# AdaLN layer with linear attention and top-2 MoE on one core: weights transposed on the host instead of on TensorE

## The reference, cut to what matters

```python
mod = (silu(c) @ wmod).reshape(4, 6, 1, -1)            # sa, ca, ga, sb, cb, gb
h = layernorm(x) * (1 + ca) + sa
QKV = einsum('bsd,ed->bse', h, W_in) + b_in            # W_in (768, 256)
Q, K = rope(Q), rope(K)
A = sum_s(K / |K| * V);  Y = A * Q @ W_out.T + b_out   # W_out (256, 256)
x = x + ga * (Y + h)
h = layernorm(x) * (1 + cb) + sb
probs = softmax(h @ router_w.T);  top 2 of 8 experts per token
out = sum_e comb[e] * ((silu(h @ Wg[e].T) * (h @ Wu[e].T)) @ Wd[e].T)   # Wg, Wu (704, 256), Wd (256, 704)
x = x + gb * (out + ...)
```

## Time and profile before

| what | value |
|---|---|
| times of three runs | 335.81, 335.94, 338.87 us |
| median | 335.94 us |
| span of the profiled execution | 338.7 us |
| the run nearest to that span | 338.87 us |
| PE, PE weight loads, DVE, ACT, POOL busy | 287.7, 196.3, 185.6, 134.1, 79.3 us |
| DMA | 33.34 MB in 25387 packets, mean 98 GB/s |

### The profile page before, as it was taken

The page is one execution under the profiler, slowest core; times in us unless marked ns, Lnnn a source line. Parts: engine busy times, 40 slices in busy tenths (PEclk is TensorE's granted clock), DMA queues, the critical chain, the costliest instruction groups (busy, mean ns, idle before and its releaser), DMA issues.

```text
span 338.7 us, 5051 instructions
## 1 busy us (share of the span) xinstructions
PE 287.7 (85%) x1466; PEld 196.3 (58%) x1467; DVE 185.6 (55%) x497; ACT 134.1 (40%) x325; POOL 79.3 (23%) x93
## 2 busy tenths in 40 slices
PE   3987799886956668999999999999999999999600
PEld 0644666775845335776777776666666666666400
DVE  1467743399368854766766763444444453444126
ACT  1273473653673055756474622223332222232000
POOL 1005544621100040022211222233222223311213
PEclk9999797999555557999999999999999999999955
DMA  7990342035353371564443110101110011100083
GB/s 247 373 291 3 132 142 85 0 90 168 87 163 116 105 219 32 154 175 140 134 154 118 31 33 32 33 20 50 28 35 31 23 31 30 44 16 0 2 261 111
DMA packets 25387, 33.34 MB, mean 98 GB/s; under 512 B 2193, under 2 KB 20276, under 8 KB 25368
## 3 DMA queue, kind: packets, MB, share of 16 engines
q1 hardware_dynamic: 22952, 27.85, 25.9%
q0 software_dynamic: 2208, 5.17, 5.3%
q10 hardware_dynamic: 208, 0.08, 0.1%
HBM read 28.86 MB, written 5.14 MB: 100 GB/s over the span
## 4 chain that ended last, share of the span: by engine, by line
PE 72%; DVE 15%; DMA 4%; ACT 3%; issue 2%; SPq 1%; POOL 0%; DVEq 0%; ACTq 0%
PE bank L750 25%; PE bank L777 19%; PE bank L561 7%; PE bank L763 5%; PE bank L631 3%; PE bank L644 3%; PE bank L551 2%; DMA W<-in_L_attn_W_in 2%; PE bank L670 2%; DMA W<-expert_parts 2%; DVE W L1097 1%; PE bank L704 1%; PE bank L738 1%; ACT W L838 1%; PE bank L570 1%
## 5 line engine op out<-in xcount | busy, mean ns | idle before, releaser
L750 PE MATMUL bank<-W,rows 128*128 x414 | 90.4, 368 | 1.1 <-DVE rows L1271 1.1
L777 PE MATMUL bank<-W,shared 128*128 (+1 forms) x276 | 69.2, 389 | 0.7 <-DVE shared L1307 0.7
L750 PEld LDWEIGHTS bank<-W,rows 128*128 128x128 f16 x414 | 40.8, 100 | 38.3 <-issue 3.6
L1282 DVE SCALAR_TENSOR_TENSOR shared<-bank,unscale,rows 128x256 f32<-128x256 f32 (+1 forms) x69 | 31.8, 461 | 53.5 <-ACT rows L945 53.4
L1381 POOL DMA_INDIRECT expert_parts<-shared,dest_i x23 | 23.3, 1014 | 149.4 <-DVE shared L1292 149.4
L777 PEld LDWEIGHTS bank<-W,shared 128*128 128x128 f32 (+1 forms) x276 | 48.2, 189 | 13.2 <-issue 8.6
L945 ACT ACTIVATE rows<-bank,unscale 128x256 f32<-128x256 f32 (+1 forms) x69 | 31.4, 454 | 45.8 <-PE bank L750 45.8
L1097 DVE SCALAR_TENSOR_TENSOR W<-bank,w_scale_bits,W 128x512 f16<-128x512 f32 (+1 forms) x48 | 33.4, 704 | 24.1 <-ACT W L853 23.8
L853 ACT ACTIVATE W<-bank,w_scale_bits 128x512 f16<-128x512 f32 (+1 forms) x48 | 30.4, 648 | 29.6 <-DVE w_scale_bits L1089 16.7
L561 PE MATMUL bank<-keep,staged 128*128 128x128 f32 x192 | 34.6, 310 | 8.0 <-DVE w_norm L1084 3.6
L561 PEld LDWEIGHTS bank<-keep,staged 128*128 128x128 f32 x192 | 26.5, 165 | 17.0 <-issue 4.9
(11 more groups left out here) (179 smaller groups left out, 322.5 us busy)
## 6 DMA issues: line engine op xcount, KB each, us to landing
staged<-in_L_ffn_Wd SPq DMA_DIRECT2D x8, 704.0 KB
staged<-in_L_ffn_Wg SPq DMA_DIRECT2D x8, 640.0 KB
staged<-in_L_ffn_Wu SPq DMA_DIRECT2D x8, 640.0 KB
W<-expert_parts SPq DMA_DIRECT2D x8, 256.0 KB, 4.6
W<-in_L_wmod SPq DMA_DIRECT2D x3, 512.0 KB, 8.1
token_rows<-rows SPq DMA_DIRECT2D x1, 1040.0 KB, 5.3
x<-in_L_attn_X SPq DMA_DIRECT2D x4, 256.0 KB, 9.0
W<-mod_rows SPq DMA_DIRECT2D x4, 256.0 KB, 4.1
```

The lines of the kernel that those rows point to most:

```text
L750: mm = pe.matmul(bank[2 + n][:, 0:2 * w], slot[:, kc * P:(kc + 1) * P], W1_16[:, bass.ds(e * (2 * W1_EXP) + at, 2 * w)], start=(k == 0), s ...
L777: mm = pe.matmul(bank[7][:, 0:D], actT[0:rows, fc * P:(fc + 1) * P], W2[0:rows, bass.ds(e * W2_EXP + fc * D, D)], start=(fc == 0), stop=(f ...
L1282: ve.scalar_tensor_tensor(act[:, n * PIECE:n * PIECE + w], bank[2 + n][:, w:2 * w], unscale[c % 2][:, 1:2], sig[:, n * PIECE:n * PIECE + w ...
```

## The change

The host now lays out all weights with the input dimension on the partitions, one contiguous run per partition. `w1[e]` holds gate and up of an expert together, 128 partitions of 2816 numbers (1.44 MB); it goes to one of two `staged` buffers. `w2[e]` (down, 0.79 MB) goes straight to its place in `W2`. Biases, router weights, condition and `wmod` come laid out too, so their transposes go, as does the `swap` matmul for the rotary pairs.

On PE only `norm(e)` is left of the groups. It is in step 1 and 2 between kv and q, in steps 6 and 7 between `th` and `r`, twice in the routing, and in tiles 2 and 3 between `down` and `turn_act`. ACT's `sum_squares(e)` is two instructions of 128x1408, its `high(e, m)` two of 128x704 from `staged`; DVE's `low(e, m)` is two of 128x704. Gate and up lie apart in `W1`, so the moving operand of a `gate_up` matmul is two runs of w columns instead of one run of 2w.

```diff
-STAGED = 4
+STAGED = 2
...
+            def load_w1(e):
+                if e >= STAGED:
+                    sp.wait_ge(s["lo_ok"], 2 * DC * (e - STAGED + 1))
+                sp.dma_start(staged[e % STAGED][:], w1_d[e]).then_inc(staged_in[e % STAGED], 16)
+            def load_w2(e):
+                wait_places(sp, e)
+                sp.dma_start(W2[:, e * W2_EXP:(e + 1) * W2_EXP], w2_d[e]).then_inc(w2_in[e], 16)
+            load_w1(0)
+            load_w1(1)
+            load_w2(0)
+            load_w2(1)
...
+            load_w2(2)
+            load_w2(3)
+            load_w1(2)
+            load_w1(3)
+            load_w2(4)
+            load_w2(5)
+            load_w1(4)
+            load_w1(5)
...
+            def norm(e):
+                pe.wait_ge(s["sumsq_ok"], 2 * (e + 1))
+                if e >= 2:
+                    pe.wait_ge(s["wscale_ok"], e - 1)
+                pe.matmul(bank[e % 2][:, 0:2], keep[:, C_ONE:C_ONE + P], sumsq[:, 2 * e:2 * e + 2],
+                          start=True, stop=True).then_inc(s["norm_done"], 1)
...
-                for g in step_slot(k, 1):
-                    turn(g)
+                if k in (1, 2):
+                    norm(k - 1)
                 for b in at_step(k, 1):                    # q
...
+                if k in (6, 7):
+                    norm(k - 4)
                 for b in at_step(k, 6):                    # r
...
                     mm.then_inc(s["cnt_done"], 1)
-                    for g in range(route_first, route_mid):
-                        turn(g)
+                    norm(4)
...
                     mm.then_inc(s["table_done"], 1)
-                    for g in range(route_mid, tiles_first):
-                        turn(g)
+                    norm(5)
...
                     for k, (slot, kc, part) in enumerate(terms):
-                        at = part * W1_EXP + kc * W1_COLS + 2 * PIECE * n
                         mm = pe.matmul(bank[2 + n][:, 0:2 * w], slot[:, kc * P:(kc + 1) * P],
-                                       W1_16[:, bass.ds(e * (2 * W1_EXP) + at, 2 * w)],
+                                       W1_pairs[:, bass.ds(e * 2 + part, 1), :, kc, n * PIECE:n * PIECE + w],
...
+                    pe.wait_ge(s["lo_ok"], 2 * DC * (c + 1))      # before gate_up of tiles 0 to 7
...
+            def high(e, m):                                       # ACT
+                sc.wait_ge(s["wscale_ok"], e + 1)
+                for kc in range(DC):
+                    at = m * W1_MAT + kc * F
+                    sc.activation(w1_part(e, 0, m, kc), staged[e % STAGED][:, at:at + F], ACT.Identity,
+                                  scale=w_scale[:, 2 * e + m:2 * e + m + 1]).then_inc(s["hi_ok"], 1)
...
-                for g in step_slot(k, 1):
-                    turn_out(g)
+                if k in (2, 3, 6, 7):                             # ACT, between ksq and q1
+                    high({2: 0, 3: 1, 6: 2, 7: 3}[k], 0)
...
+                if k in (2, 3, 6, 7):                             # ACT, after wA
+                    high({2: 0, 3: 1, 6: 2, 7: 3}[k], 1)
...
+                if k in (1, 5, 6, 9):                             # ACT, end of the step
+                    sum_squares({1: 1, 5: 2, 6: 3, 9: 4}[k])
             sc.wait_ge(s["sub_ok"], 1)
             sc.activation(expo[:], logit_less_max[:], ACT.Exp).then_inc(s["expo_ok"], 1)
+            sum_squares(5)
+            high(4, 0)
+            high(4, 1)
+            high(5, 0)
+            high(5, 1)
...
+                    if c in (1, 2):                               # ACT, tile c, after slots_out
+                        sum_squares(c + 5)
+                    if c in (3, 5):
+                        high(c // 2 + 5, 0)
...
+                if k in (3, 4, 7, 8):                             # DVE, between kv and q
+                    low({3: 0, 4: 1, 7: 2, 8: 3}[k], 0)
...
+                if k in (1, 2, 6, 7):                             # DVE, before y
+                    power_scale({1: 0, 2: 1, 6: 2, 7: 3}[k])
...
+                if k in (3, 4, 7, 8):                             # DVE, between diff and h2
+                    low({3: 0, 4: 1, 7: 2, 8: 3}[k], 1)
...
             routing_choice(ve, link)
+            power_scale(4)
             routing_places(ve, link)
             routing_table(ve, link)
-            for g in range(route_first, tiles_first):
-                turn_out(g)
+            power_scale(5)
+            low(4, 0)
+            low(4, 1)
...
+                if first and c in (0, 4, 6):                      # DVE, tile c, after slots_out
+                    low({0: 5, 4: 6, 6: 7}[c], 0)
...
                 ve.tensor_copy(actT[:, 0:4 * P], bank[5][:]).then_inc(s["actT_v"], 1)
+                if first and c in (0, 4, 6):
+                    low({0: 5, 4: 6, 6: 7}[c], 1)
```

More of the change, by code:

```diff
@@ L279, in layer @@
         staged_in = [sem(f"staged_in{r}") for r in range(STAGED)]
+        w2_in = [sem(f"w2_in{e}") for e in range(E)]
         xs_in = [sem(f"xs_in{r}") for r in range(4)]
@@ L283, in layer @@
         part_in = [sem(f"part_in{b}") for b in range(B)]
-        groups = [("w_in", None, n) for n in range(3)] + [("w_in_swapped", None, 0), ("w_out", None, 0)]
-        FIRST = len(groups)
-        groups += [("norm", 0, 0)]
-        for e in range(E):
-            groups += [("gate", e, n) for n in range(3)] + [("up", e, n) for n in range(3)]
-            groups += [("down", e, n) for n in range(3)] + [("norm", e + 1, 0)] * (e + 1 < E)
-        MATRIX = {"gate": 0, "up": 1, "down": 2}
-        STEPS = 10
@@ L320, in layer @@
-        for g in range(tiles_first, ALL_GROUPS):
-            group_bank[g] = (g - route_mid) % 2
-        def last_on_bank(g):
-            before = [h for h in range(g) if group_bank[h] == group_bank[g]]
-            return before[-1] if before else None
-        def tile_slot(i, c, n):
-            if not (isinstance(i, int) and i == 0 and c < len(TILE_GROUPS)):
-                return range(0)
-            at = tiles_first + sum(map(sum, TILE_GROUPS[:c])) + sum(TILE_GROUPS[c][:n])
-            return range(at, at + TILE_GROUPS[c][n])
@@ L335, in split @@
-        def split(g):
-            return groups[g][0] in ("gate", "up")
-        def by_act(g):
-            return split(g) or (g < FIRST and g % 2 == 0) or (groups[g][0] == "down" and g < tiles_first)
-        def by_dve(g):
-            return split(g) or not by_act(g)
-        def wait_turned(eng, upto):
-            eng.wait_ge(s["turn_act"], sum(by_act(g) for g in range(upto)))
-            eng.wait_ge(s["turn_dve"], sum(by_dve(g) for g in range(upto)))
-        def wait_out(eng, g):
-            by = by_dve if by_dve(g) else by_act
-            eng.wait_ge(s["turn_dve" if by_dve(g) else "turn_act"], sum(by(h) for h in range(g + 1)))
@@ L787, in tile_step @@
             def tile_step(i, c):
-                def turn_some(n):
-                    for g in tile_slot(i, c, n):
-                        turn(g)
                 if isinstance(i, int) and i == 0 and c < E:
-                    done = tile_slot(0, c, 0).start
-                    if c == 0:
-                        for h in range(route_first, route_mid):
-                            wait_out(pe, h)
-                    need = [g for g in range(done) if groups[g][0] in ("gate", "up") and groups[g][1] <= c
-                            or groups[g][0] == "down" and groups[g][1] < c]
-                    wait_turned(pe, need[-1] + 1)
-                gate_up(i, c, turn_some)
+                    pe.wait_ge(s["lo_ok"], 2 * DC * (c + 1))
+                gate_up(i, c)
                 if not (isinstance(i, int) and c == SLOT_TILES - 1):
@@ L843, in turn_out @@
-            def turn_out(g):
-                kind, e, n = groups[g]
-                if (kind, n) == ("down", 1) and e + 1 < E:
-                    sum_squares(e + 1, 1)
-                if split(g):
-                    if (kind, n) == ("gate", 0):
-                        sc.wait_ge(s["wscale_ok"], e + 1)
-                    sc.wait_ge(s["turn_done"], g + 1)
-                    src, hi, lo = split_views(g)
-                    c = 2 * e + MATRIX[kind]
-                    sc.activation(hi, src, ACT.Identity, scale=w_scale[:, c:c + 1]).then_inc(s["turn_act"], 1)
-                    if (kind, n) == ("gate", 2) and e + 1 < E:
-                        sum_squares(e + 1, 0)
-                elif by_act(g):
-                    if kind == "down" and n == 0:
-                        wait_places(sc, e)
-                    sc.wait_ge(s["turn_done"], g + 1)
-                    evacuate(copy, g).then_inc(s["turn_act"], 1)
@@ L910, in _ @@
                     else:
-                        sc.wait_ge(s["turn_act"], sum(by_act(g) for g in range(FIRST)))
+                        sc.wait_ge(s["wout_in"], 16)
                     for dc in range(DC):
```

425 lines of the change are left out of this document (115 added, 310 removed).

## The result

The changed kernel takes 320.06 us (median of four runs, 319.35 to 321.41) against 337.4 us for the kernel before beside it (335.81 to 340.68): a ratio of 0.9466, 95% interval 0.94 to 0.9532. The profiled execution took 321.41 us with a span of 319.6 us; the span before was 338.7 us. Between the medians the gain is 17.3 us, between the two profiled executions 19.1.

The account below looks back on a forecast made before the run. PE was taken as the bound from tile 1 on. Tiles -15.3, everything before routing -3.0, routing +2.2 and table to tile 0 -2.4 made -18.5 us, from the median 335.94 to about 317.5 us; range 312 to 324.

Parts of the forecast that it names:

- PE is the bound and a group costs 0.42 to 0.50 us: From tile 1 on PE is busy throughout; each transposed group there costs it 0.42 to 0.50 us.
- Tiles, -15.3: Tiles 0 to 7 without groups take 64.3 instead of 79.6 us, including 3.5 of waiting before tile 7.
- Prices of the new work: In the tiles: 948 ns per DVE low half, 0.84 us per ACT high half, 1.37 us per squares instruction.
- Head, -0.5: Head and steps 1 and 2: earlier kv, but q(0) waits for squares; net -0.5 us, from -2.5 to +1.
- Steps 2 to 9, -3.0 with everything ahead: Everything before routing, head included: fewer groups against new waits; routing starts 3.0 us earlier, bounds -6 to +3.
- Routing, +2.2: Routing: `power_scale(4)` before `routing_places` waits for norm(4) on PE, so DVE goes on 2.2 us later.
- Table to tile 0, -2.4: From dest_i to the first gate matmul: the gather is left, covering the new halves; 2.4 us less.
- Sum: Whole kernel: -15.3 - 3.0 + 2.2 - 2.4 = -18.5 us, a span of 320.2 us.
- (a), the clock: Attention: more PE idling; kv and q of batches 2 and 3 at half clock, 7 us: 324.5; chance 0.12.
- (b): Tiles: new ACT and DVE work lies on PE's way; all 24 us, half gives 329; chance 0.05.
- (c): `gate_up` matmuls slower reading two runs; at 80 ns more each, 351 us; chance 0.03.
- (d): More gain: w1(0) lands early, tile 7's wait is hidden, attention gives 5 us: 311; chance 0.12.

Follow-up runs that it names:

- e4: Changed kernel with 43 groups of four transposes, results read by nobody, put back on PE in tiles 0 to 7: 337.4 us, ratio 0.9977.
- e1: Changed kernel with the high and low halves of expert 7 made one tile earlier: 316.62 us, ratio 0.9351.
- e6: Changed kernel with PE loading the expert's number before it waits for DVE's low half, not after: 319.94 us, ratio 0.9458.
- e8: Changed kernel with norm(0) and norm(1) moved behind q, so q doesn't wait for ACT's squares: 318.36 us, ratio 0.9429.
- e2: Changed kernel with `power_scale(4)` moved behind `routing_places`: 319.35 us, ratio 0.9428.
- e7: Changed kernel with 50 transposes, read by nobody, filling PE's gap before the sums of step 2: 318.5 us, ratio 0.9408.
- e3: Changed kernel with six float32 matmuls of 128x512, read by nobody, filling PE's gap before the sums of step 2: 318.79 us, ratio 0.9401.

## Why the prediction was right, and where it was off

The predicted time was 317.5 us as a ratio of 0.945 to the median before; 0.9466 was measured. The predicted span was 320.2 and the measured one 319.6. That the two spans agree to 0.6 us is in part luck: the tiles gave 1.5 us less than forecast and what stands ahead of them 2.0 more. The terms, by their own steps:

- **PE is the bound and a group costs 0.42 to 0.50 us.** Right for the tiles; e4 puts 43 groups back, and in tiles 1 to 6, where PE is full, they cost 0.43 us each.
- **Tiles, -15.3.** Measured 79.63 - 65.88 = -13.75. Tile 0 took 8.62 (8.5 predicted), the wait before tile 7 3.16 (3.5), tiles 1 to 6 7.4 to 7.6 (7.37, and for norm in two of them 0.2 where 0.35 was predicted). What was missed is what the wait does to the matmuls behind it: 5.42 instead of 3.73 us. The sum priced the wait and left PE at full clock after it. This is the term that was mis-sized, by 1.9 us; e1 gives it back together with the wait.
- **Prices of the new work.** 948 ns for a low half was 966, 840 for a high half 870, 1366 for squares 1368. Reading SBUF instead of PSUM was neither dearer nor cheaper beyond that, and extrapolating along columns from the earlier trace rows was good to 4%.
- **Head, -0.5.** q(0) was forecast at 24.8 behind the squares, and came at 23.81. w1(0) was there at 20.69: the early end of the bounds. The rule quoted in the prediction from the Trainium skill, "DMA: Bandwidth & Descriptors", section Bandwidth, that loads want to be of at least 1 MiB, made the early end the likelier; the trace agrees in the outcome, with squares that start at 20.69 behind the 1.44 MB load. That the size of the load is the cause is not shown: the changed kernel moves most of its loads in other pieces, at 381 GB/s from 9 to 20 us where the earlier trace rows had 358, and no run varies a size. kv(0) came later than forecast (20.07 for 18), which hid the wait for norm in this profile; e6 and e8 show that it is there otherwise, and worth up to 3.2 us.
- **Steps 2 to 9, -3.0 with everything ahead.** Measured -5.0, inside the bounds of -6 to +3. The round trip in step 6 came as predicted (1.04 us idle at 76.06 for 1.3). h2(3) ended at 89.2 (89 to 90.5), and the routing started 5.3 us later, for the 5.5 that were predicted. So of the 2.0 us between -3.0 and -5.0 at least part is an addition: 89 to 90.5 and 5.5 make 94.5 to 96, and the prediction wrote 96.5.
- **Routing, +2.2.** +2.17 measured; e2 takes 1.6 of it away by moving the one call.
- **Table to tile 0, -2.4.** -2.31; the gather is ahead of the tile and covers the halves.
- **Sum.** -5.0 + 2.17 - 2.31 - 13.75, and -0.2 from the rest, make -19.1 against -18.5. The tiles gave 1.5 less and the head and attention 2.0 more.

Of the rivals, **(a), the clock**, was right in its mechanism and wrong in its extent. In step 3 it struck the sums and kv, not q nor step 4, and cost about 3 us in place of 7, hidden in a total that came out better elsewhere. The kernel before paid there too: behind its 3.63 us of idle, q(1) took 4.01 us where q(0) took 2.75. It also struck y of batch 3 (3.52 us; 1.89 in the kernel before), which cost next to nothing: in the three profiles where y stayed warm (e1, e7, e8) DVE waited 0.87 us for norm(2), in the first 1.04. The reason that the prediction gave against it did not hold as a rule. From the stretch at 90.9 to 97.2 it read that transposes do not hold the clock up; in e7 fifty of them did. The clock in that stretch was low for a reason that no run here settles. In part the rival was also the missing term of tile 7. **(b)** fell but for tile 7: tiles 1 to 6 have PE busy throughout, and in e1 tile 7 as well. **(c)**, two runs in the moving operand, fell: 18 matmuls take 3.73 us before and after. **(d)** did not come by itself, but the profiles of e1 and e8 show gains of the kind it named: the wait of tile 7 is 5 us with its aftermath, not 3.5.

The Trainium skill, "TensorE: Matmul & The Clock Gate", section "Why this matters for your kernels", which wants no long idle gaps between bursts of matmuls, was the better guide here: the trace agrees, with 6.1 us idle and then a granted clock of 0.57 over 8.5 us, and e3 and e7 undo it by filling the gap.

## What to carry to other kernels

When an engine that bounds the kernel gives work away, price each wait that is left on it twice: once for its length, and once for the matmuls behind it, which here could run at half clock and then took 1.7 to 2.3 us more. The second price is not certain: behind gaps of 2.0 to 2.7 us it was paid in some executions and not in others. Work that moves to idle engines is free only until the first use of its result, so order it by due time: of the eight experts' halves one was late, and it cost 5 us beside a gain of 19. And take times of steps from several profiles when a start scatters, as kv(0)'s does here by 3 us: two profiles that differ in such a start can't price a change behind it.
